# Score products of four attention layers on four 32-row strips in two phases, with four buffers of masked keys in three of the layers

## The reference

```
h = split_heads(queries @ Wq); k, v = the same of ctx with Wk, Wv     # (8, 16, 128, 8)
scores = einsum('bhqd,bhkd->bhqk', q, k) / sqrt(8)
scores = where(scores == 0, -1e30, scores)       # layer 0: an exact zero is a mark
                                                 # layer 1: where(mask, scores, -1e10)
                                                 # layers 2, 3: neither, but biases on q, k, v
attn = softmax(scores, axis=-1)
out = einsum('bhqk,bhkd->bhqd', attn, v) -> (8, 128, 128);  x = x + out @ Wo (+ bias)
x = x + ffn(layernorm(x))                        # a different one in each layer
```

## Time and profile before

| | us or share |
|---|---|
| profiled execution, its own time | 878.3 |
| its span | 876.5 |
| median of three runs | 879.82 |
| TensorE busy | 721.6 (82%) |
| VectorE busy | 438.7 (50%) |
| ScalarE busy | 284.7 (32%) |
| GpSimd busy | 291.4 (33%) |
| mean granted TensorE clock | 0.928 of full speed |

### The profile page before, as it was taken

How to read it: one execution, slowest core, us unless ns; L and a number is a source line. 1 busy time by engine, 2 the same in 40 slices (tenths; PEclk the granted TensorE clock), 3 DMA queues, 4 the chain that set the end, 5 groups by cost and what they waited for, 6 DMA issues and landing times.

```text
span 876.5 us, 15643 instructions
## 1 busy us (share of the span) xinstructions
PE 721.6 (82%) x6143; PEld 433.4 (49%) x6169; DVE 438.7 (50%) x1182; ACT 284.7 (32%) x477; POOL 291.4 (33%) x324
## 2 busy tenths in 40 slices
PE   6799915999997898998787998787967987797774
PEld 3365612774554575655444565344524543453443
DVE  5566487663445775655454555533253334324332
ACT  3233310123332514442153343233314422333332
POOL 7212211222211322322655221343264226433442
PEclk9999966999999879998798999999998899999998
DMA  6900060040000000000215300120111012111212
GB/s 136 328 6 2 26 192 7 19 165 29 1 1 1 0 1 1 1 1 1 58 26 149 83 1 2 43 34 31 40 33 35 22 34 40 34 35 29 34 32 67
DMA packets 43759, 39.03 MB, mean 45 GB/s; under 512 B 11648, under 2 KB 34720, under 8 KB 43560
## 3 DMA queue, kind: packets, MB, share of 16 engines
q1 hardware_dynamic: 37240, 26.88, 10.6%
q0 software_dynamic: 5120, 10.50, 5.4%
q10 hardware_dynamic: 1328, 0.66, 0.3%
HBM read 30.75 MB, written 7.27 MB: 43 GB/s over the span
## 4 chain that ended last, share of the span: by engine, by line
PE 67%; DVE 14%; issue 8%; DMA 4%; another core or an unknown queue 2%; POOL 2%; ACT 2%; DVEq 0%; SPq 0%; POOLq 0%; ACTq 0%
PE psum L1615 9%; PE psum L1638 8%; PE psum L548 8%; PE psum L506 7%; PE psum L1625 5%; PE psum L570 4%; PE psum L495 3%; PE psum L582 2%; PE psum L709 2%; PE psum L1201 2%; PE psum L591 2%; PE psum L1182 2%; DVE scr L929 1%; DVE scr L895 1%
## 5 line engine op out<-in xcount | busy, mean ns | idle before, releaser
L289 POOL TENSOR_TENSOR scr<-KT,hmask 128x512 f32<-128x512 f32 x64 | 67.7, 1064 | 158.0 <-PE psum L548 63.2
L1483 DVE COPY scr<-psum 128x512 f32<-128x512 f32 x64 | 44.3, 692 | 136.0 <-PE psum L1625 88.2
L406 DVE TENSOR_REDUCE Mp<-psum 128x8 f32<-128x1024 f32 x64 | 78.5, 1226 | 63.8 <-PE psum L506 27.5
L313 ACT ACTIVATE scr<-psum 128x1024 f32<-128x1024 f32 x64 | 65.5, 1023 | 120.4 <-PE psum L548 44.7
L463 PE MATMUL psum<-fill,identb 128*128 128x512 bf16 x300 | 78.6, 401 | 1.9 <-issue 1.2
L548 PE MATMUL psum<-Qa,scr 64*128 64x128 f32 x1024 | 73.9, 284 | 0.0
L506 PE MATMUL psum<-scr 64*128 64x512 f32 x256 | 71.8, 638 | 0.0
L548 PEld LDWEIGHTS psum<-Qa,scr 64*128 64x128 f32 x1024 | 63.3, 188 | 15.6 <-issue 10.4
L1625 PEld LDWEIGHTS psum<-ident,scr 128*128 128x128 f32 x304 | 33.9, 148 | 65.1 <-issue 57.1
L1615 PE MATMUL psum<-KT,xsT 128*64 128x512 f32 x120 | 35.7, 668 | 31.2 <-issue 31.2
L1365 POOL DMA_INDIRECT yb_d<-scr,tok x44 | 42.8, 972 | 54.9 <-ACT scr L1313 49.4
(11 more groups left out here) (345 smaller groups left out, 1248.5 us busy)
## 6 DMA issues: line engine op xcount, KB each, us to landing
big<-in_L_ffn_W SPq DMA_DIRECT2D x2, 2048.0 KB, 9.0
big<-in_L_ffn_W SPq DMA_DIRECT2D x8, 512.0 KB, 9.6
big<-in_L_ffn_W SPq DMA_DIRECT2D x1, 4096.0 KB, 13.5
b1r<-in_L_ffn_b SPq DMA_DIRECT2D x1, 2048.0 KB, 10.9
scr<-yb_d SPq DMA_DIRECT2D x6, 256.0 KB, 3.1
xn_d<-xn SPq DMA_DIRECT2D x2, 512.0 KB, 3.2
scr<-ya_d SPq DMA_DIRECT2D x4, 256.0 KB, 3.0
yb_d<-scr,tok POOLq DMA_INDIRECT x44
```

The source lines that it names most:

```text
L289: pool.tensor_tensor(Km[:, i % 2, c, :, :], KT[:, c, i, :].unsqueeze(1).to_broadcast([P, HV, P]), hmask4[:, :].unsqueeze(2).to_broadcast([ ...
L313: act.activation(PT[i % 2][:, c, :], pair(weights_unit(i, c)), ACT.Exp, scale=SCALE).then_inc(S(f"exp{c}"), 1)
L406: dve.tensor_reduce(Mp[:, HC * c:HC * c + HC, DH:DH + 1], pair(scores_unit(i, c)).rearrange("p (j k) -> p j k", j=HC), AX.X, ALU.max, nega ...
L1483: ins = dve.tensor_copy(hTg[:, g % 2, :], bank[[3, 6][g % 2]])
```

## The change

The scores of a tile are now computed by `score_strips(i, n)`, in two phases n = 0 and 1. A phase has four products, one in each strip of 32 rows, each over two of the four key copies (256 columns): phase 0 takes strips 0 and 2 of half 0 and strips 1 and 3 of half 1, phase 1 the other strips. The four products of a phase go to four PSUM banks; phase 1 writes the other half of each bank's columns. Phase 1 waits for `scores_half`, which the end of phase 0 signals. The other two key copies hold only zeros in a strip's rows, so each strip multiplies half as many columns as before.

For that both halves of the next tile must be ready at once: phase 0 waits for `km_ready0` and `km_ready1`. Phase 1 stands ahead of the weights of half 0. The PSUM pairs are dealt out anew, and with them the wait for `exp1` moves from the scores to the weights of half 0. At the layer's start, both phases stand behind the waits for the second quarter of the copied queries and for the copied values. The masked keys have four buffers in layers 1 to 3: `Km` for tiles with `i % 4` below 2, and `Kx`, the space of `ind`, for the others; GpSimd then waits for the weights four tiles back. In layer 0 there are two buffers as before. The diff:

```diff
--- before.py
+++ after.py
@@ -149,6 +149,7 @@
         hmask = sb("hmask", [P, HC])
         hmask4 = sb("hmask4", [P, HV])
         ind = sb("ind", [P, 2, 2, HC * P], BF16)
+        Kx = ind[:, :, :, :].rearrange("p a c n -> p (a c n)").bitcast(F32).rearrange("p (u c v k) -> p u c v k", u=2, c=2, v=HV)
         half = sb("half", [P, B])
         spare = sb("spare", [P, 1])
         stats = sb("stats", [P, B, 6])
@@ -261,15 +262,18 @@
         VB = {2: 0, 3: 1}
         OB = {1: 0, 2: 1, 3: 2}
         def scores_unit(i, c):
-            return 2 * ((4 * i - 2 + 2 * c if i else c) % 3)
+            return 2 * ((4 * i - 2 + c if i else c) % 3)
 
         def weights_unit(i, c):
-            return 2 * ((4 * i + 3 + 2 * c) % 3)
+            return 2 * ((4 * i + 4 + c) % 3)
 
         def pair(u):
             return psum[:, u:u + 2, :].rearrange("p a n -> p (a n)")
 
         PAD = [("wq", 0, 0), ("wk", 0, 1), ("wq", 2, 2), ("wk", 2, 3), ("wq", 3, 4), ("wk", 3, 5)]
+
+        def masked_keys(L, i):
+            return (Km if L == 0 or i % 4 < 2 else Kx)[:, i % 2]
 
         def pool_rstd(pool, link, n, i):
 
@@ -284,9 +288,10 @@
             for i in tiles:
                 for c in range(2):
                     pool.wait_ge(S("k_copied"), 4 * L + 2 * (i // 4) + c + 1)
-                    if i >= 2:
-                        pool.wait_ge(S(f"weights_ps{c}"), n0 + i - 1)
-                    pool.tensor_tensor(Km[:, i % 2, c, :, :], KT[:, c, i, :].unsqueeze(1).to_broadcast([P, HV, P]),
+                    kept = 4 if L else 2
+                    if i >= kept:
+                        pool.wait_ge(S(f"weights_ps{c}"), n0 + i - kept + 1)
+                    pool.tensor_tensor(masked_keys(L, i)[:, c, :, :], KT[:, c, i, :].unsqueeze(1).to_broadcast([P, HV, P]),
                                        hmask4[:, :].unsqueeze(2).to_broadcast([P, HV, P]), ALU.mult
                                        ).then_inc(S(f"km_ready{c}"), 1)
 
@@ -495,23 +500,33 @@
                 return pe.matmul(bank[4 + n], w[:, L, HC * c:HC * c + HC, :].rearrange("p h r -> p (h r)"),
                                  src[:, 512 * h:512 * h + 512], start=True, stop=True)
 
-            def scores(i, c):
-                pe.wait_ge(S(f"km_ready{c}"), n0 + i + 1)
-                if i > 1:
-                    pe.wait_ge(S(f"exp{c}"), n0 + i - 1)
-                if i == 1 and c == 1:
-                    pe.wait_ge(S("max1"), n0 + 1)
-                u = scores_unit(i, c)
-                for r in range(2):
-                    ins = pe.matmul(bank[u + r], QT[64 * r:64 * r + 64, c, i, :],
-                                    Km[64 * r:64 * r + 64, i % 2, c, :, :].rearrange("p v k -> p (v k)"),
-                                    start=True, stop=L > 1, skip_group_check=L < 2)
-                if L == 1:
-                    for r in range(2):
-                        ins = pe.matmul(bank[u + r].rearrange("p (j k) -> p j k", j=4), identb[:, :],
-                                        fill[:, i, :].unsqueeze(1).to_broadcast([P, 4, P]),
-                                        start=False, stop=True, skip_group_check=True)
-                ins.then_inc(S(f"scores{c}"), 1)
+            def score_strips(i, n):
+
+                if n == 0:
+                    for c in range(2):
+                        pe.wait_ge(S(f"km_ready{c}"), n0 + i + 1)
+                    if i > 1:
+                        pe.wait_ge(S("exp0"), n0 + i - 1)
+                else:
+                    pe.wait_ge(S("scores_half"), n0 + i + 1)
+                for c in range(2):
+                    for s in (c ^ n, (c ^ n) + 2):
+                        rows = slice(32 * s, 32 * s + 32)
+                        v = 2 * (s % 2)
+                        ins = pe.matmul(bank[scores_unit(i, c) + s // 2][:, P * v:P * v + 2 * P], QT[rows, c, i, :],
+                                        masked_keys(L, i)[rows, c, v:v + 2, :].rearrange("p v k -> p (v k)"),
+                                        start=n == 0, stop=L > 1, skip_group_check=True)
+                    if n == 1 and L != 1:
+                        ins.then_inc(S(f"scores{c}"), 1)
+                if n == 0:
+                    ins.then_inc(S("scores_half"), 1)
+                elif L == 1:
+                    for c in range(2):
+                        for r in range(2):
+                            ins = pe.matmul(bank[scores_unit(i, c) + r].rearrange("p (j k) -> p j k", j=4), identb[:, :],
+                                            fill[:, i, :].unsqueeze(1).to_broadcast([P, 4, P]),
+                                            start=False, stop=True, skip_group_check=True)
+                        ins.then_inc(S(f"scores{c}"), 1)
 
             def mask_zeros(i, c):
                 pe.wait_ge(S(f"zeros{c}"), i + 1)
@@ -536,16 +551,14 @@
                 if c == 0:
                     pe.wait_ge(S("qa_ready"), n0 + i + 1)
                     if i > 0:
-                        pe.wait_ge(S("max1"), n0 + i + 1)
+                        pe.wait_ge(S("exp1"), n0 + i)
                 elif i + 1 < B:
                     pe.wait_ge(S("max0"), n0 + i + 2)
-                else:
-                    pe.wait_ge(S("exp1"), n0 + i)
                 u = weights_unit(i, c)
                 for v in range(HV):
                     for r in range(2):
                         rows = slice(64 * r, 64 * r + 64)
-                        ins = pe.matmul(bank[u + r][:, P * v:P * v + P], Km[rows, i % 2, c, v, :], Qa[rows, c, :],
+                        ins = pe.matmul(bank[u + r][:, P * v:P * v + P], masked_keys(L, i)[rows, c, v, :], Qa[rows, c, :],
                                         start=v == 0, stop=L > 1, skip_group_check=True)
                 for r in range(2):
                     if L == 0:
@@ -618,12 +631,11 @@
             queries(1)
             pe.wait_ge(S("k_copied"), 4 * L + 3)
             turn(1)
-            pe.wait_ge(S("q_copied"), 4 * L + 1)
-            scores(0, 0)
-            queries(2)
             pe.wait_ge(S("q_copied"), 4 * L + 2)
             pe.wait_ge(S("v_copied"), L + 1)
-            scores(0, 1)
+            score_strips(0, 0)
+            queries(2)
+            score_strips(0, 1)
             queries(3)
             pe.wait_ge(S("q_copied"), 4 * L + 4)
             if L == 0:
@@ -635,17 +647,17 @@
                 if here:
                     turn_maxima(i)
                 if ahead:
-                    scores(i + 1, 0)
+                    score_strips(i + 1, 0)
                 if i > 1:
                     turn_outputs(i - 2)
+                if ahead:
+                    score_strips(i + 1, 1)
                 if i > B:
                     unread(pe, 5, 3)
                 if here:
                     weights(i, 0)
-                if ahead:
-                    if L == 0:
-                        mask_zeros(i + 1, 0)
-                    scores(i + 1, 1)
+                if ahead and L == 0:
+                    mask_zeros(i + 1, 0)
                 if 0 < i <= B:
                     attend(i - 1, 0)
                 if i > 1:
```

## The result

The changed kernel is slightly slower. Its median is 886.3 us (880.4 to 891.2 in 20 runs) against 880.1 us (875.9 to 888.4 in 20 runs) for the kernel before, run beside it. The ratio is 1.006 with a 95% interval of 1.004 to 1.008, so about 0.6% or 5.3 us (the medians differ by 6.2). The forecast was no change, 875 to 885. The profiled execution takes 888.2 us, 9.9 more than that of before, at a mean granted clock of 0.90 (0.93 before).

A forecast was written before the change was run, and what follows sets the result against it. TensorE was taken to bound the kernel (67% of the chain). Layer 0 +8.3, layer 1 -5.25, layers 2 and 3 -3.1 sum to -0.05 us, so 879.8, no change; range 875 to 885, 8 in 10 runs 870 to 890.

The forecast's parts named there:

- The phase of four strips: Score products, all layers: four 256-column products in four row strips run together, 0.65 us a phase against halves of 1.06 and 0.96.
- rival (a): Score phases: strips run only two at a time, 1.06 a phase, 903 us (0.07), or partly together, 885 to 888 (0.10).
- Layers 2 and 3: Inner tile: TensorE waits 0.43 us for VectorE's normalised outputs; tile 6.66 instead of 6.85; -1.55 per layer, both -3.1.
- Layer 1: Inner tile stays bound by TensorE, no wait; about -0.75 us on 8.89, tile 8.1; whole layer -5.25.
- Layer 0's inner tile: Waits of 1.1 us for GpSimd's keys and 0.8 for VectorE's marks; tile 9.95, five tiles +5.5.
- Rival (c): Layers 0, 2 and 3: the waits placed on VectorE are absent; -9 us, 870.5; chance of faster 0.15.
- all three waits: Layers 2 and 3: 0.43 us for normalised outputs; layer 0: 1.1 for GpSimd's keys and 0.8 for VectorE's marks.
- is bound by VectorE in both, 0: Layer 0, tile 0: VectorE sets its length before and after the change, so it adds 0 us.
- +1.6: Layer 0, tile 1: the same two waits as inner tiles with less work to cover them, +1.6 us.
- +1.15: Layer 0's start: both phases wait for the copied values, +1.96 us, less two times 0.41 for shorter phases.
- Rival (b): Layer 0: waits make TensorE's clock fall, 1 to 1.7 us each; about six falls, one a tile, give 888 to 892; chance 0.13.
- the argument against it: Layer 0's new tile: TensorE is still busy 80% of it, as in many stretches at full clock.

## Why the prediction was wrong

**What held.** The phase of four strips is 0.65 us, as taken, and its four products start within 0.02 us of each other; rival (a) is out in both of its forms. The Trainium skill, "TensorE: Matmul & The Clock Gate", Part 3, gives 3.07 times for four row strips; from it the prediction worked out an estimate of 0.56 for the passes. With the 0.2 taken for filling and emptying that would be a phase of 0.76, and 0.65 was measured, so the measurement decides for full overlap here. Layers 2 and 3: the wait for VectorE is there, 0.35 where 0.43 was worked out, the tile 6.64 to 6.65 where 6.66 was. Layer 1: 8.12 against 8.1, 5.35 us less against 5.25. Together these three layers gave 8.1 us off the time of the whole where 8.35 was forecast. Layer 0's inner tile: waits of 1.06 and 0.66 against 1.1 and 0.8, 10.01 against 9.95. Rival (c) is out, since all three waits exist. One inner tile took 10.39, because GpSimd began its key 0.38 late; that was not foreseen and is small.

**The step that failed** is the price of layer 0's start and first tiles. The sum says of tile 0 "is bound by VectorE in both, 0", of tile 1 "+1.6", and of the start "+1.15". With full clock on both sides these are close to right: tile 0 needs 8.47 with the new form and 7.94 with the old one, tile 1 9.57 and 7.92, the start 0.9 more, and layer 0 as a whole 9.2 against 8.3. But the sum priced both kernels at one clock. In the profiled pair the three terms came to +3.0, +4.5 and +3.3. The rows of before, 9.37 for tile 0 and a granted clock of 0.72 in 28 to 34, were from a stretch that had already lost its clock once, for 3.4 us. The change makes this same stretch worse: a new wait of 1.86 ahead of it, one of 2.45 for one of 1.39 behind it, and each fall slows the work that VectorE waits for. Within the first 60 us the low level lasted 23.9 us in the profiled execution, against 3.4 before, and 10 to 17 us in the others without products in all the waits. That costs 5 to 9 us, where before it cost 1.3, and it is the distance between forecast and result: with the clock kept up the changed kernel is at 0.997 of before, and no change was forecast.

**Rival (b) named the mechanism, and its place and price were wrong.** It said "One fall costs 1 to 1.7 us and changes little" and looked for one fall per tile in all tiles. The inner tiles, busy 8.23 of 10.01 with waits of 1.06 and 0.66, keep full clock, as the argument against it said. The rival had noted the wait that brings the new fall, "tile 0 one of about 2.4", and gave it the price of a short fall. For the fall of before that price is right (1.3); the falls of the changed kernel cost 5 to 9 together. And it did not ask what becomes of the fall that was there already.

The terms together: -8.1 for layers 1 to 3, +7.9 for layer 0's new waits against a kernel before that has its own short fall, and +5 to +6 for the clock in most profiled executions give +5 to +6, or 0.6 to 0.7%; 0.6% was measured. That layer 0's waits came to 7.9 where 8.3 was forecast is partly luck: with full clock on both sides they are 9.2, and 1.3 of that is hidden by the fall that the kernel before had.

## What to carry to other kernels

Price a wait on TensorE by the clock it may cost as well as by its length, and do so first in the stretch where the trace of before already shows a granted clock under full: there a wait that grew from 1.39 to 2.45 us, with a new one of 1.86 ahead of it that mattered less, went with a loss of 5 to 9 us, while waits of 1 us in busy tiles cost only themselves. A few unread products in such waits tell whether the clock is the cause, and are a cure too. When a product is moved ahead of the release of the buffer it reads, count the buffers in each layer apart: a tile of layer 1 became 0.77 us shorter with four and 0.36 longer with two. Time saved on the bounding engine soon becomes a wait on the next one, whose order is then the thing to edit.

## What the runs showed of the hardware

Four products on four 32-row strips run side by side in f32: they start within 0.02 us of each other, and 4 x 256 columns take 0.65 us, against 1.06 for two products of 512 on two strips of 64 rows. A fall of the clock is not of one length: 3.4, 6.8 and 10.2 us were seen at the same place, and all of them vanished with 32 products of 512 columns in the waits. The same kernel took 6% longer in the first runs (879 to 880 us) than on two other chips (827 and 829). By the profiles nearly all of it is in the last mixture stage, where VectorE's copies (L1495) had 36 to 48 us of idle time in each of the six profiles from the slower runs, waiting for what the trace calls remote, and none in the seven from the two faster chips; the cause of that is open.
